# Exponentials of the attention in two ScalarE instructions over two PSUM banks each, in place of four over one bank

## What is computed

```python
def _attend(q, k, v):                       # in blocks 0, 1 and 2, five times in all
    attn = jnp.einsum('bhnd,bhsd->bhns', q, k) * SCALE
    attn = jax.nn.softmax(attn, axis=-1)    # the exponentials of this case
    o = jnp.einsum('bhns,bhsd->bhnd', attn, v)
...
x = x + g_sa * (_attend(q, k, v) @ sa_proj_w + sa_proj_b)   # self attention
x = x + _attend(q, k_ctx, v_ctx) @ ca_proj_w + ca_proj_b    # cross attention
x = x + g_ff * (gelu(xm @ fc1_w + fc1_b) @ fc2_w + fc2_b)
```

## Time and profile before

| what | value |
|---|---|
| time, median of 3 runs (lowest, highest) | 1867.91 us (1866.65, 1868.31) |
| the profiled execution: its own time, its span | 1866.06 us, 1864.3 us |
| TensorE busy | 94% of the span |
| VectorE busy | 88% |
| ScalarE busy | 74% |
| exponentials, L1211 | 640, in sets of four |
| granted TensorE clock | 0.996 of full speed |

### The profile page before, as it was taken

One profiled execution on the slowest core, in us unless ns is written; L12 is line 12 of the kernel. 1 busy time (PEld: TensorE's weight loads), 2 busy tenths in 40 slices (PEclk: granted clock), 3 DMA queues, 4 the chain that ended last, 5 costly groups with the idle time before them and its releaser, 6 DMA issues.

```text
span 1864.3 us, 88096 instructions
## 1 busy us (share of the span) xinstructions
PE 1756.0 (94%) x38181; PEld 1502.5 (81%) x38181; DVE 1639.4 (88%) x4236; ACT 1383.1 (74%) x3340; POOL 643.9 (35%) x1145
## 2 busy tenths in 40 slices
PE   3788999999999999999999999999999999999898
PEld 3577788888788888888888888888888888877788
DVE  2898889899899999999999999989999989998874
ACT  1465678787778778777877787878777777777697
POOL 1432323333423333333333333333333333432341
PEclk9899999999999999999999999999999999999999
DMA  4200000000000000000000000000000000000000
GB/s 162 71 14 9 17 23 9 17 23 23 23 23 14 16 19 23 23 23 23 9 17 23 23 23 23 23 3 23 23 23 23 23 13 18 20 11 9 8 5 15
DMA packets 57165, 42.62 MB, mean 23 GB/s; under 512 B 13520, under 2 KB 55632, under 8 KB 56528
## 3 DMA queue, kind: packets, MB, share of 16 engines
q1 hardware_dynamic: 56784, 36.99, 6.8%
HBM read 32.51 MB, written 4.46 MB: 20 GB/s over the span
## 4 chain that ended last, share of the span: by engine, by line
PE 74%; DVE 14%; ACT 6%; issue 3%; DMA 0%; POOL 0%; SPq 0%; DVEq 0%; POOLq 0%
PE half L981 9%; PE half L881 8%; PE half L861 7%; PE half L900 7%; PE half L885 7%; PE half L928 5%; PE half L918 5%; DVE top L1070 4%; PE half L802 4%; PE half L990 4%; PE half L848 4%; PE half L911 3%; PE half L833 3%; PE half L837 3%; ACT pT L1246 2%
## 5 line engine op out<-in xcount | busy, mean ns | idle before, releaser
L761 POOL TENSOR_TENSOR shifted<-moments,eps 128x2 f32<-128x2 f32 x256 | 50.6, 198 | 1027.1 <-DVE moments L1037 1027.0
L1211 ACT ACTIVATE pT<-half 128x512 f32<-128x512 f32 x640 | 328.0, 610 | 102.3 <-PE half L885 101.2
L1070 DVE TENSOR_REDUCE top<-half 128x32 f32<-128x2048 f32 x160 | 365.1, 2282 | 29.4 <-PE half L861 27.8
L881 PE MATMUL half<-o_rows,of_keys 32*128 32x128 f32 x5120 | 273.8, 281 | 5.1 <-ACT o_rows L1163 3.0
L885 PE MATMUL half<-q_heads,k_heads 32*128 32x128 f32 x5120 | 261.4, 271 | 3.0 <-issue 2.9
L1246 ACT ACTIVATE pT<-half,mod 128x64 f32<-128x64 f32 x896 | 196.1, 332 | 50.6 <-PE half L981 49.5
L881 PEld LDWEIGHTS half<-o_rows,of_keys 32*128 32x128 f32 x5120 | 205.9, 186 | 26.3 <-issue 11.5
L885 PEld LDWEIGHTS half<-q_heads,k_heads 32*128 32x128 f32 x5120 | 207.8, 187 | 5.4 <-issue 5.4
L1191 ACT ACTIVATE k_heads<-half,key_bias,own_head_sb 128x256 f32<-128x256 f32 x320 | 163.4, 571 | 47.8 <-PE half L837 46.2
L861 PE MATMUL half<-k_heads,q_heads 32*128 32x128 f32 x5120 | 187.9, 281 | 9.5 <-issue 5.0
L1043 DVE TENSOR_SCALAR n_rows<-x_rows,moments,rstd 128x128 f32<-128x128 f32 x512 | 189.0, 416 | 3.9 <-POOL rstd L763 3.0
(11 more groups left out here) (151 smaller groups left out, 3745.0 us busy)
## 6 DMA issues: line engine op xcount, KB each, us to landing
gates<-gate_store SPq DMA_DIRECT2D x128, 128.0 KB, 3.1
x_rows<-x SPq DMA_DIRECT2D x32, 128.0 KB, 2.2
c_rows<-context SPq DMA_DIRECT2D x32, 128.0 KB, 2.5
out<-x_rows SPq DMA_DIRECT2D x32, 128.0 KB, 1.8
w_sb<-weights SPq DMA_DIRECT2D x1, 2368.0 KB, 12.7
pT<-weights SPq DMA_DIRECT2D x1, 1024.0 KB, 4.7
logit_bias<-logit_store SPq DMA_DIRECT2D x64, 1.5 KB, 3.4
row_sb<-rows SPq DMA_DIRECT2D x1, 769.5 KB, 6.4
```

Of the source, the lines that this page charges most:

```text
L881: nc.tensor.matmul(halves[HALF_OF[n]][:, g, tb * D:(tb + 1) * D], of_keys[part, 2 * tb:2 * tb + 2, :], low[s][part, :], start=True, stop=F ...
L1070: nc.vector.tensor_reduce(top[s][:, :].rearrange("p (g c) -> p g c", c=32)[:, :, 0:2 * GROUP], halves[HALF_OF[n]][:, :, :].rearrange("p g ...
L1211: nc.scalar.activation(turn_cols[s][:, g, :], halves[HALF_OF[n]][:, g, :], ACT.Exp, scale=ATT_SCALE).then_inc(scores_read, 1)
```

## The change

In `scores`, ScalarE's loop over the four banks becomes a loop over two pairs. The first instruction waits until two banks are filled, reads the 1024 columns of banks 0 and 1, writes 1024 columns of `pT`, and raises `scores_read` by two at its end. The second does the same with banks 2 and 3. TensorE's waits, the order of steps, the plan of banks and everything else are as before.

```diff
                     if kind == "scores":
 
-                        for g in range(TURNS):
-                            attended += 1
+                        for g in range(0, TURNS, 2):
+                            attended += 2
                             act.wait_ge(scores_filled, attended)
-                            nc.scalar.activation(turn_cols[s][:, g, :], halves[HALF_OF[n]][:, g, :], ACT.Exp, scale=ATT_SCALE).then_inc(scores_read, 1)
+                            nc.scalar.activation(turn_cols[s][:, g:g + 2, :], halves[HALF_OF[n]][:, g:g + 2, :], ACT.Exp,
+                                                 scale=ATT_SCALE).then_inc(scores_read, 2)
```

## The result

The changed kernel takes 1946.01 us against 1868.11 us before, each the median of four runs; the ratio is 1.0409, with a 95% interval of 1.0382 to 1.0437. One of the four runs, 2488 us at a granted clock of 0.656, was disturbed and is left out of the ratio. The forecast was 1872.3 us, with 1876.5 as its upper end. It named the sign and missed the size by a factor of 17.

A forecast was written before the change was run, and what follows sets the result against it. TensorE, busy 94% of the span, was taken as the bound, not ScalarE. Late banks 6.0 + 0.8 less 1.0 gained made 5.8 us, a quarter off +4.4: from 1867.91 to 1872.3 us, range 1866.5 to 1876.5.

The forecast's parts named there:

- What it adds: a wait for the second bank: First exponential of a set: needing banks 0 and 1, it starts 0.04 us later where ScalarE waits for the scores.
- right behind a table load: Eight of 18 chain stretches of four exponentials, where ScalarE was taken as itself late; each set ends 0.08 us earlier.
- The mechanism that the prediction did put first: Banks come free later, bank 0 by 0.44 to 0.48 us, so TensorE's fills stall; 6.0 + 0.8 us, chance 0.60.
- 738.99 kind: Four places where TensorE fills bank 0, possible at 1.22 us after the set's start: 0.23 us late at one, 0.41 at three.
- The prediction's 20 places: TensorE fills that come late: 16 places on the chain, 6.0 us, and four with the chain on VectorE, half counted, 0.8 us.
- a quarter off: Part of the 5.8 us taken as given back, where stalls replace chain time called issue; leaves +4.4 us.
- the two places priced at 1.18: Bank 0 fills like that at 243.59 with ScalarE late: at 0.74 us, possible at 1.18, so 0.44 us late each.
- 549 kind: Three places where fills of bank 0 and soon after bank 2 come late; the larger delay stands, 0.43 us each.
- 709 kind: Four places with bank 0 fills 0.41 us late while the chain is on VectorE; half counted, 0.8 us.
- The gain of 1.0 us: Sets on the chain end earlier with two instructions fewer: 8 x 0.08 + 10 x 0.04 us.
- the dear bank's edge: Rival: a two-bank exponential costs as much as two, 1.09 us; 8 us slower, 1875.9 us; chance 0.05.
- ScalarE's relief: Rival: sets end earlier, so later ScalarE work feeds TensorE sooner; 13 us freed, at most 4.3 on the path, 1863.6 us; chance 0.08.

## Why the prediction was wrong, and where it was right

**The step that failed** is "What it adds: a wait for the second bank". It priced the wait at the 0.04 us that bank 1 is filled after bank 0, which the trace bears out (a median of 42 ns), and said that nothing on ScalarE's queue is behind this wait that doesn't profit from the earlier end. The table load is on that queue. In the kernel before it ran ahead of the wait, since the wait was part of the exponential; in the changed one it is behind it. The prediction read the 8 chain stretches "right behind a table load" as cases where ScalarE was late anyway, and took for granted that the load would stay where it was. No term of the sum, and none of the rivals, held a table load that starts late; the diff has it in the small print, `then_inc(scores_read, 2)`.

What that was worth can be worked out from the traces. The 75 loads take 96.2 us in all. Before, by the times at which `scores_filled` rose, 39 of them were through when bank 0 of their scores was filled, and the 36 others had 12.8 us left between them: 83.4 us were under cover of the scores. After, all 96.2 us come behind the fill. So 83.4 us more lie between scores and exponentials, and the span grew by 1943.1 - 1864.3 = 78.8 us. The chain shows that most of it counts: before it runs through eight of these loads whole and one in part, 11 us, and after through 59 of the 75, 75 us. In the chain after, a load is not named but is the "issue" between the last scores and the exponentials, as here ahead of the `tops` at 609.23:

```profile
605.53 0.34 PE half L885 x8
605.94 1.21 issue
607.15 1.95 ACT pT L1211 x2
609.23 1.17 PE half L861 x32
```

ScalarE's idle time says where, and not how much: it is 110.5 us ahead of the loads and 90.1 us ahead of the exponentials, against 1.3 us and 102.3 us before. That is 97 us more, but an engine with 22 us less work in a span 78.8 us longer idles 101 us more whatever the cause. TensorE was busy for 94% of the span before, so little slack was there to take the stretch up, and that is the second half of the lesson: the `tops` at 609.23 stands idle for 1.28 us, as long as the load takes.

**The mechanism that the prediction did put first is real**, and the kernel of pairs that raise by one shows it with the table loads back in their place. A fill of bank 0 was to be possible at 1.18 us after a set's start when ScalarE is late and at 1.22 when it waits for bank 1. Both places shown below waited for the scores, so 0.04 of the 1.22 lies ahead of their start, and 1.18 was to be seen. Here is one of the 738.99 kind, 743.53 to 744.70, and its twin a period earlier:

```profile
410.59 1.07 PE L879 MATMUL half<-k_heads,q_heads 32*128 32x128 f32 x32
410.82 1.94 ACT L1229 ACTIVATE pT<-half 128x1024 f32<-128x1024 f32 x2 [1.21 <-PE half L903]
411.99 0.68 PE L929 MATMUL half<-w_sb,kvT 128*128 128x128 f32 x4 [0.33 <-ACT pT L1229]
...
743.53 1.94 ACT L1229 ACTIVATE pT<-half 128x1024 f32<-128x1024 f32 x2 [1.20 <-PE half L903]
744.70 0.68 PE L929 MATMUL half<-w_sb,kvT 128*128 128x128 f32 x4 [0.19 <-ACT pT L1229]
```

The fill comes 1.17 us after the set's start, at both. In this whole trace the matmuls of steps other than `tops`, `scores` and `values` wait 8.7 us for exponentials, in 29 waits, where before none did. The prediction's 20 places have 6.0 + 4 x 0.41 = 7.6 us, and it named nine more that it did not count. Where single exponentials raise only at the end of each second one, the same fill comes at 1.23:

```profile
411.93 2.06 ACT L1229 ACTIVATE pT<-half 128x512 f32<-128x512 f32 x4 [1.16 <-PE half L903]
413.16 0.68 PE L929 MATMUL half<-w_sb,kvT 128*128 128x128 f32 x4 [0.35 <-ACT pT L1229]
```

The sum of the prediction was +5.8 us with nothing given back and +4.4 us after a quarter off. For the pairs that raise by one it came to 1868.38 x 0.0019 = 3.5 us, with an interval of 0.9 to 6.0 us. Both values are in it, so the quarter can't be judged. For late banks without pairs the prediction's list has to be redone: the set starts no later, bank 0 can be filled at 0.49 + 0.60 + 0.14 = 1.23 us and bank 2 at 2.06 + 0.14 = 2.20 us. That adds 0.05 us at the two places priced at 1.18, 0.04 at the three of the 549 kind and 0.01 at the eleven others, 6.3 us, and 0.8 us for the 709 kind: 7.2 us with the fractions kept, within the measured 6.2 to 13.4. The quarter that I took off on record, to 5 us, made the forecast of that run worse. That the place decides agrees with the kernel that pairs only where the half is taken whole: it shows no loss. Its interval overlaps that of the pairs everywhere a little (up to 1.0014, from 1.0005), so these two runs alone would not prove it. The gain of 1.0 us worked out from the chain lies within the interval of that run and is not shown.

**The other terms.** A set takes 1.94 us where I took 1.98, below the lower bound of 1.96: two instructions fewer save 2.06 - 1.94 = 0.12 us, 0.06 each. The pair takes 1.02 us against 1.04. The Trainium skill, "ScalarE: Activation LUTs", section "What ACT_TABLE_LOAD costs", gives 186 ns beside 0.833 ns a column; 1024 columns would take 1.04 us, an estimate from that page, and the rows have 1024 ns. Its 0.19 us a set is further off than the 0.08 that I took. Of the rivals, the dear bank's edge did not occur. ScalarE's relief did (22 us less work), and was worth nothing that the runs show. Of what was to be seen in the profile, the 320 exponentials and their length came true, and the stalled fills in the kernel of pairs that raise by one. ScalarE's busy time fell by 22 us and not by 10 to 16. The waits for exponentials were to be 14 us or more; they are 67.3, nearly all of it from the late table loads: with these back in place they are 13.1.

## What to carry to other kernels

Before pricing a change to an instruction that waits, look at what is placed right in front of it on its engine and needs none of what it waits for: here a table load of 1283 ns that was under cover of the scores, 39 times in 75 wholly, as long as the wait was inside the exponential. Raising a semaphore by two instead of one, or giving an instruction a second wait, moved the wait into an instruction of its own ahead of that load; count in steps of one where a table load may stand ahead, and look for an event-semaphore row on the line of the wait and for idle time ahead of ACT_TABLE_LOAD. Where the separate wait had to stay, an exponential of one column ahead of it brought the load forward, and 0.6% was left of 4.1%. And an instruction that covers two banks gives both back at its end: paired only where the next user takes both, it cost nothing here, and gained nothing that the runs can tell.

## What the runs showed of the hardware that was not expected

A wait that is an instruction of its own costs little by itself: 85 of them 0.15% (0.03 to 0.28%), where 75 ahead of a table load cost 3.9%. The Trainium skill, "Perfetto Trace Analysis", section "Identifying Dependency Chains", notes that an instruction that waits on several engines may get EventSemaphore instructions in front of it; the kernel with a second wait agrees (74 added waits, 74 such instructions), and here they came for a single wait as well, once the instruction raised its semaphore by two, 320 times in 320. That they come from the form of the raise is shown by the kernels that differ in nothing else; whether the chip could hold both in one instruction is not shown by any run.

A ScalarE instruction over two PSUM banks of 512 columns each showed no cost at the bank's edge: 1024 ns for 1024 columns, beside 610 ns for 512 over one bank, which leaves (1024 - 610) / 512 = 0.81 ns a column. From 256 to 512 columns within a bank it was (610 - 392) / 256 = 0.85 ns.
